# Feed-forward rows turned by VectorE and five DMAs instead of by TensorE

## The reference

```python
def reference(X, W_Q, W_K, W_V, w_gate, w_up, w_down):
    x = X                                             # (8, 2048, 256)
    n = layernorm(x)
    Q, K, V = xpos(n @ W_Q), xpos(n @ W_K, downscale=True), n @ W_V
    p = softmax(Q @ K.T) * 0.9 ** abs(row - column)   # per sequence
    x = x + p @ V
    n = layernorm(x)
    gate, y = fp4_linear(n, w_gate), fp4_linear(n, w_up)      # 704 columns
    return x + fp4_linear(silu(gate) * y, w_down)
```

## Time and profile before

| what | value |
|---|---|
| median of 3 runs | 2549.67 us (2548.38 to 2549.73) |
| profiled execution, first to last instruction | 2546.6 us |
| what lies around this span, against the median | 3.1 us |
| granted TensorE clock, mean over the span | 0.999 of full speed |
| busy: PE, PEld | 2518.4, 2290.0 us |
| busy: DVE, ACT, POOL | 2140.9, 1489.8, 1816.8 us |
| DMA | 203.27 MB, mean 80 GB/s |

### The profile page before, as it was taken

The page is one execution under the profiler, slowest core; times in us unless marked ns, Lnnn a source line. Parts: engine busy times, 40 slices in busy tenths (PEclk is TensorE's granted clock), DMA queues, the critical chain, the costliest instruction groups (busy, mean ns, idle before and its releaser), DMA issues.

```text
span 2546.6 us, 51904 instructions
## 1 busy us (share of the span) xinstructions
PE 2518.4 (99%) x16160; PEld 2290.0 (90%) x16160; DVE 2140.9 (84%) x4759; ACT 1489.8 (59%) x2966; POOL 1816.8 (71%) x1929
## 2 busy tenths in 40 slices
PE   8999999999999999999999999999999999999997
PEld 7888879999999999999999999999999999999996
DVE  8999878888878888888888888888888888888886
ACT  5766565656555655566565656565556655555654
POOL 6999956667767676667766776677666776677665
PEclk9999999999999999999999999999999999999999
DMA  8878511122111311131112111131113111211110
GB/s 285 302 271 299 186 50 30 34 86 66 38 40 45 107 37 42 34 106 42 42 34 91 62 38 40 45 107 39 42 34 106 41 42 34 95 58 38 40 38 22
DMA packets 163473, 203.27 MB, mean 80 GB/s; under 512 B 15184, under 2 KB 116752, under 8 KB 163216
## 3 DMA queue, kind: packets, MB, share of 16 engines
q1 hardware_dynamic: 163216, 200.01, 24.1%
HBM read 103.42 MB, written 77.59 MB: 71 GB/s over the span
## 4 chain that ended last, share of the span: by engine, by line
PE 85%; POOL 0%; DVE 0%; issue 0%; ACT 0%; POOLq 0%
PE score L516 27%; PE acc L655 19%; PE ring L516 19%; PE acc L516 9%; PE ring L622 6%; PE ring L675 3%; PE acc L697 1%; PE ring L613 1%; DVE hT L1226 0%; POOL probs L998 0%; ACT probs L823 0%; ACT hT L793 0%; POOL h_buf L1019 0%; POOL xv L1004 0%; POOL h_buf L1013 0%
## 5 line engine op out<-in xcount | busy, mean ns | idle before, releaser
L516 PE MATMUL score<-keys,q_st 128*128 128x512 f32 x3072 | 733.7, 394 | 3.0 <-ACT probs L823 2.6
L516 PEld LDWEIGHTS score<-keys,q_st 128*128 128x128 f32 x3072 | 567.0, 188 | 117.8 <-issue 3.0
L998 POOL TENSOR_TENSOR probs<-probs,decay 128x512 f32<-128x512 f32 (+3 forms) x416 | 450.7, 1097 | 197.5 <-ACT probs L823 197.5
L655 PE MATMUL acc<-vals,pT 128*128 128x256 f32 x3984 | 554.6, 286 | 0.8 <-DVE pT L1226 0.8
L516 PE MATMUL ring<-w_gu,xqT 128*128 128x512 f32 (+1 forms) x2304 | 509.1, 374 | 0.0
L655 PEld LDWEIGHTS acc<-vals,pT 128*128 128x128 f32 x3984 | 498.1, 189 | 7.3 <-DVE pT L1226 2.0
L516 PEld LDWEIGHTS ring<-w_gu,xqT 128*128 128x128 f32 x2304 | 419.0, 188 | 63.6 <-DVE xqT L1226 0.4
L793 ACT ACTIVATE xqT<-ring 128x256 fp32r<-128x256 f32 x128 | 49.3, 385 | 706.9 <-PE ring L613 706.9
L1239 DVE TENSOR_REDUCE smax<-score 128x1 f32<-128x1024 f32 x256 | 312.8, 1222 | 95.6 <-PE score L516 94.1
L1226 DVE TENSOR_TENSOR pT<-ring,pT 128x512 fp32r<-128x512 f32 (+3 forms) x432 | 248.7, 600 | 66.7 <-ACT pT L793 65.5
L1004 POOL TENSOR_TENSOR xv<-xv,xe 128x256 f32<-128x256 f32 x128 | 94.4, 737 | 269.1 <-DVE xv L1079 269.1
(11 more groups left out here) (133 smaller groups left out, 4470.0 us busy)
## 6 DMA issues: line engine op xcount, KB each, us to landing
k_dram<-keys SPq DMA_DIRECT2D x56, 512.0 KB, 4.5
keys<-k_dram SPq DMA_DIRECT2D x56, 512.0 KB, 7.3
edge<-vals SPq DMA_DIRECT2D x288, 64.0 KB, 2.1
q_raw<-q_dram SPq DMA_DIRECT2D x129, 128.0 KB, 2.6
x_in<-X SPq DMA_DIRECT2D x32, 512.0 KB, 4.5
q_dram<-q_stage SPq DMA_DIRECT2D x32, 512.0 KB, 5.4
x_res<-X SPq DMA_DIRECT2D x128, 128.0 KB, 2.1
out<-x_res SPq DMA_DIRECT2D x128, 128.0 KB, 1.7
```

The source lines that it names most:

```text
L516: mm = pe.matmul(dst, stat(a, k), mov(m, k), start=i == 0, stop=ends and i == n - 1)
L655: mm = pe.matmul(pv_out, pT[g % 2][:, a, j * P:(j + 1) * P], edge[places[m]][:] if kb in edges else vals[m][:, kb, :], start=i == 0, stop= ...
L998: op = pool.tensor_tensor(probs[:, k0:k1], probs[:, k0:k1], decay[:, off + k0:off + k1], ALU.mult)
```

## The change

The transposes of the quantised feed-forward rows leave PE, and with them their two uses of a ring bank in each step. In their place, for tile t:

- DVE in step t+4 (`h_turned_blocks`, behind the lower parts of the last group of probabilities) turns the 128x768 rows in blocks of 32 by 32, each within its own 32 partitions, and writes them to `h_turn`. `hq` has one buffer now, and `h_turn` takes the place of the second.
- SP (`rows_turned`) waits for that, writes `h_turn` to DRAM in one DMA of 384 KB, waits until it has landed, and reads it back into `hqT` in four DMAs of 96 KB, each into 32 partitions, in runs of 768 bytes. This stands in SP's step ahead of the loads of values and edges, of the store and of the load of X, and behind `load_keys` for the second half of the keys and `load_q`.
- ACT in step t+5 makes the upper part from `hqT` in one instruction of 768 columns, behind the first two groups of probabilities instead of ahead of the exponentials.
- DVE in step t+5 makes the lower part in one instruction (`h_lower`), between the lower parts of the first two groups and the maximum of the second half of the scores. Both of its inputs lie in SBUF; before, one lay in PSUM.
- POOL's write to `hq` waits for the turn of the tile before instead of for PE's transposes. Tile 0 takes its 8 blocks as 4 and 4 instead of 2, 3 and 3.

```diff
@@ plan_slots @@
-            for h in range(2):
-                if g == min(max(len(gs) - LATER, 0) + h, max(len(gs), 1) - 1) and has(s - LAG):
-                    take("hT", s - LAG, h)
@@ SP @@
+            def rows_turned(j, t):
+
+                g, i = j * T + t, t % 2
+                sp.wait_ge(h_turned, g + 1)
+                passed()
+                if t > 1 or not isinstance(j, int) or j:
+                    sp.wait_ge(h_split, g - 1)
+                    passed()
+                sp.dma_start(h_dram[i], h_turn.rearrange("p (c r) -> p c r", c=CT)).then_inc(turn_out, 16)
+                sp.wait_ge(turn_out, (g + 1) * 16)
+                for c in range(CT):
+                    sp.dma_start(hqT[i][c * QUAD:(c + 1) * QUAD, :, :], h_dram[i, :, c, :].rearrange("(a i) r -> i a r", a=CT)).then_inc(hqT_back[i], 16)
...
                 if s + 2 <= T or more and not last:
                     load_q(j, s + 2, more)
+                if s >= TURNED or not is_first:
+                    rows_turned(j, s - TURNED)
@@ PE down @@
-                    copied(at, "hT", t, 1)
+                    pe.wait_ge(h_split, tile(at, t) + 1)
@@ ACT @@
             def h_transposed(at, t):
                 if has(at, t):
-                    for h, n in enumerate((CT, HK - CT)):
-                        upper(hT[0][:, h * CT:h * CT + n, :].rearrange("p k t -> p (k t)"),
-                              bank(at, "hT", t, h)[:, 0:n * P], at, "hT", t, h)
+                    act.wait_ge(hqT_back[t % 2], halves(at, t) * CT * 16)
+                    if has(at, t - 1):
+                        act.wait_ge(dn_done, tile(at, t))
+                    act.activation(chunks(hT[0][:]), quads(hqT[t % 2][:]), ACT.Copy).then_inc(h_upper, 1)
...
                 attend(at, s - 1, range(min(n, 2)))
+                h_transposed(at, s - LAG)
@@ DVE @@
+            def h_turned_blocks(at, t):
+                if has(at, t):
+                    dve.wait_ge(hq_ready, tile(at, t) + 1)
+                    if has(at, t - 1):
+                        dve.wait_ge(turn_out, tile(at, t) * 16)
+                    dve.transpose(h_turn.rearrange("p (c k j) -> p k c j", c=CT, j=QUAD), hq.rearrange("p (k c i) -> p k c i", c=CT, i=QUAD)).then_inc(h_turned, 1)
+
+            def h_lower(at, t):
+                if has(at, t):
+                    dve.wait_ge(h_upper, tile(at, t) + 1)
+                    dve.tensor_tensor(chunks(hT[1][:]), quads(hqT[t % 2][:]), chunks(hT[0][:]).bitcast(F32), ALU.subtract).then_inc(h_split, 1)
...
                 attend(at, s - 1, range(min(n, 2)))
+                h_lower(at, s - LAG)
                 maxima(at, s, 1)
...
                 attend(at, s - 1, range(2, n))
-                for h in range(2):
-                    h_transposed(at, s - LAG, h)
+                h_turned_blocks(at, s - TURNED)
                 h_levels(at, s - 3)
```

More of the change, by code:

```diff
@@ L46 @@
 RING = 3
-XR, LAG, LATER = 8, 5, 3
+XR, LAG, TURNED = 8, 5, 4
+QUAD = 32
 W_SLOTS = 3
@@ L89, in groups @@
     bs = blocks_of(t)
-    size = CT if 0 < t < T - 1 else CT - 1
+    size = CT if t < T - 1 else CT - 1
     first = len(bs) % size or size
@@ L170, in build @@
         silu = he
-        hq = [hq_buf[:, i * FT:(i + 1) * FT] for i in range(2)]
+        hq, h_turn = (hq_buf[:, i * FT:(i + 1) * FT] for i in range(2))
         xv, xe, xq = sb("xv", [P, D]), sb("xe", [P, D]), sb("xq", [P, D])
@@ L223, in build @@
         probs = sb("probs", [P, L])
+        hqT = [sb(f"hqT{i}", [P, CT, HK * QUAD]) for i in range(2)]
         score = ctx.enter_context(nc.psum_tensor("score", [P, 4, CH], F32))
@@ L256, in build @@
         hq_step, hv_ready, hg_ready, hq_ready = sem("hq_step"), sem("hv_ready"), sem("hg_ready"), sem("hq_ready")
+        sp_passed, h_turned, turn_out, hqT_back, h_upper, h_split = sem("sp_passed"), sem("h_turned"), sem("turn_out"), [sem(f"hqT_back{i}") for i in range(2)], sem("h_upper"), sem("h_split")
         NSTEP_W, NSTEP_LN2, NSTEP_XQ, NSTEP_HQ = 5, 2, 6, 5
@@ L502, in _ @@
                 step(B - 1, s, False, False)
-            for t in range(T - LAG, T):
-                store(B - 1, t)
+            for s in range(T, T + LAG):
+                if s - TURNED < T:
+                    rows_turned(B - 1, s - TURNED)
+                store(B - 1, s - LAG)
             for i in range(XR):
@@ L663, in attend @@
                         group(at, t, g + 2)
-                    for h in range(2):
-                        if g == min(max(len(gs) - LATER, 0) + h, len(gs) - 1):
-                            later(h)
-            def h_transposed(at, t, h):
-                if has(at, t):
-                    for ks in (range(0, CT), range(CT, HK))[h:h + 1]:
-                        if h == 0:
-                            pe.wait_ge(hq_ready, tile(at, t) + 1)
-                        dst = slot(at, "hT", t, h)
-                        for j, k in enumerate(ks):
-                            mm = pe.transpose(dst[:, j * P:(j + 1) * P], hq[t % 2][:, k * P:(k + 1) * P], ident[:])
-                        mm.then_inc(filled, 1)
             def gate_up(at, t):
@@ L999, in decays @@
                     op.then_inc(decayed, 1)
+                if len(groups(s)) <= 2:
+                    meanwhile()
             def x_quantised(at, t):
@@ L1252, in attend @@
                     lower(pT[g % 2][:, 1, 0:n], bank(at, "pT", t, g)[:, 0:n], pT[g % 2][:, 0, 0:n], at, "pT", t, g)
-            def h_transposed(at, t, h):
+            def h_turned_blocks(at, t):
                 if has(at, t):
-                    for n in (CT, HK - CT)[h:h + 1]:
-                        hi, lo = (hT[i][:, h * CT:h * CT + n, :].rearrange("p k t -> p (k t)") for i in range(2))
-                        lower(lo, bank(at, "hT", t, h)[:, 0:n * P], hi, at, "hT", t, h)
+                    dve.wait_ge(hq_ready, tile(at, t) + 1)
+                    if has(at, t - 1):
+                        dve.wait_ge(turn_out, tile(at, t) * 16)
[4 more added lines that the diff above has]
+                    dve.tensor_tensor(chunks(hT[1][:]), quads(hqT[t % 2][:]), chunks(hT[0][:]).bitcast(F32), ALU.subtract).then_inc(h_split, 1)
             def residual(at, t):
```

23 lines of the change are left out of this document (14 added, 9 removed).

## The result

| what | before | after |
|---|---|---|
| median | 2549.64 us (4 runs, 2548.38 to 2549.73) | 2621.23 us (4 runs, 2618.21 to 2622.3) |
| ratio, with its 95% interval | | 1.0281 (1.0267 to 1.0296) |
| span of the profiled execution | 2546.6 us | 2618.3 us |
| granted TensorE clock, mean | 0.999 | 0.987 |

The change made the kernel 72 us slower. The forecast was +23, with 2618 as its upper end.

A forecast was written before the change was run, and what follows sets the result against it. PE, busy 99%, was taken as the bound. Terms: -84 (transposes) + 63 (third-group waits) + 32 (batch ends) + 12 (tail) = +23 us on the 2546.6 us span; with 3.1 us around it, forecast 2572, range 2522 to 2618.

The forecast's parts named there:

- PE loses the transposes: PE's stream: series of four 0.44 us and of two 0.22, so 0.66 a tile times 128, 84 us saved.
- waits at the third group, and the rest: PE, arriving earlier, waits for DVE's delayed lower part of the third probability group: 63 us, between 21 and 111.
- ends of a batch: Edges queue behind keys and turned rows; PE waits 3.9 us plus clock loss: seven ends, 32 us (18 to 45).
- tail: After the last scores, two ways through DRAM in series, some 21 us for 9: 12 us more (8 to 15).
- the forecast's own list of waits: PE's wait at the third group, tile by tile, from 1.16 us (tile 14) to 0.06 (tile 11); 7.9 a batch.
- d = 0.7: Delay in us of DVE's second maximum caused by the split ahead of it; possible between 0.2 and about 1.3.
- the forecast's rule: DVE instruction with two SBUF inputs and POOL instruction reading SBUF exclude each other throughout; split not 0.95 us beside busy POOL.
- Rival B: Split reaches DVE as POOL passes between instructions, delaying the second maximum only 0.2 to 0.35 us: 2513 to 2542; chance 0.27.
- What DVE and ACT gain and lose: DVE drops 0.68 + 0.43 us, takes a 0.95 us turn where it waited anyway; ACT's single instruction is free.
- The way through DRAM: Turned rows written and read back by SP in 8.0 us, write 3.3; covered by 2.5 us in normal steps.
- rival D: Way through DRAM takes over 10.5 us, late in each step, 100 us and more: 2610 to 2700; chance 0.08.
- the 0.7 us taken: At each batch end, PE's lower clock after the wait for edges costs 0 to 1.5 us more, 0.7 taken.

The follow-up runs named there:

- before_fewer_transposes: Kernel before the change, with PE making only the first transpose of each of its two series of feed-forward rows (four of six dropped); 2511.57 us.
- exps_late: Changed kernel, nothing left out, with six idle ACT copies of 128 columns added ahead of the exponentials; 2604.57 us.
- split_late: Changed kernel with DVE's split of the turned rows moved behind the last group's lower part instead of ahead of the second maximum; 2697.82 us.
- pool_split: Changed kernel with the split (lower part of the turned rows) made on POOL, ahead of its decays, instead of on DVE; 2654.14 us.

## Why the forecast had the right sign and too small a size

The four terms of the sum, with what each came to. The first is read from steps without waits, the third and the fourth from the lengths of the steps above. The second is what is left of the 71.7 us between the two spans, so it holds everything else, and its agreement with the forecast shows nothing by itself.

| term | forecast | found |
|---|---|---|
| PE loses the transposes | -84 | -45 (0.35 x 128) |
| waits at the third group, and the rest | +63 | +66 |
| ends of a batch | +32 | +33.5 |
| tail | +12 | +17.5 |
| sum | +23 | +72 |

**What PE loses** is the step that failed: "That is 0.66 us a tile, times 128 tiles = 84 us." It took the length of two pieces of the chain for what their removal gives. 0.35 us a tile was measured, in steps without waits of the changed kernel and of its variants, and before_fewer_transposes, in which nothing is added and four of six are left out, gave 38 us. In the table this is 39 of the 49 us between the sums. But the same 0.66 us also stood in the times at which PE was to reach the third group, and there it made the waits too long. With 0.36 us for the series of four and nothing for the series of two, the forecast's own list of waits at d = 0.7 gives 5.3 us a batch for 7.9, so 42 us for 63. The step that failed put right alone would have made the sum -45 + 42 + 32 + 12 = +41, 18 us more. The other 31 us are 24 at the waits, 1.5 at the ends of a batch and 5.5 in the tail.

**What the third group waits for** came out as worked in its mechanism: PE waited 54.5 us for pT (forecast 40 to 80), the split's mean was 1.44 us (forecast 1.2 to 2.0), and the second maximum came 0.74 us later, where d = 0.7 was taken. That the second input in SBUF is the cause was shown from both sides (45 us off, 41 on). With this the forecast's rule is borne out as well: the Trainium skill, "SBUF — State Buffer", section "Who interferes with whom", says that a VectorE instruction with two inputs in SBUF contends with a GpSimd instruction that reads SBUF, and that one with at most one input there does not, outside the modes in which VectorE uses two ports. The runs agree, with 1490 ns against 968 for the same columns in the same place. Rival B, POOL clear of the split, would have needed a mean near 0.95.

That the term's size agrees is luck, though: 21 us too much, from the price of the transposes, stood against 24 us that the working didn't have. It reasoned that with ACT's earlier exponentials "PE's scores and POOL's decay have more lead than before", and put their cost at nothing. They bring POOL's decays onto DVE's levels of h, and to put the exponentials back gave 17 us in exps_late. This is a second step that failed. The 17 us don't come through the second maximum, which starts at C+6.51 in exps_late too. PE's waits for pT fell by 6.7 us there, to 47.8, and those for the residual sum from 6.8 to 2.5; the trace doesn't name the rest. Some 7 us of the 66 are not accounted for. One run alone gives the 17, and exps_late moves all that follows the exponentials, so this is no exact split.

By tile the waits are not where the list had them, either. Tile 1 (step 2) waited 2.1 us a batch where 1.04 were forecast, tile 12 (step 13) 0.85 for 0.43, and tile 13 (step 14) for nothing, where 0.79 were forecast.

**What DVE and ACT gain and lose.** The turn took 969 ns (0.95 taken). Its place "where DVE waited anyway" was right for PE's wait, and wrong for what is behind it: split_late and pool_split showed that the residual sum is a second deadline. DVE's busy time from 1000 to 2400 us rose from 1169.5 to 1280.9 us, and ACT and POOL now wait for DVE's mean and variance in most steps.

**The way through DRAM** was covered in normal steps, as worked; ACT waited for its rows 11 times, 41.3 us in all. The write landed after 2.3 us at the median (3.3 taken), so rival D had no ground.

**The end of a batch** went as written in six of seven cases. SP's issues there, to be read beside the earlier trace rows:

```profile
1416.46 3.48 SPq L446 DMA_DIRECT2D keys<-k_dram  x4
1420.14 0.44 SPq L490 DMA_DIRECT2D h_dram<-hq_buf  x1
1430.00 1.74 SPq L493 DMA_DIRECT2D hqT<-h_dram  x4
1432.00 0.36 SPq L455 DMA_DIRECT2D v_raw<-v_dram  x1
1432.41 1.17 SPq L470 DMA_DIRECT2D edge<-vals  x2
```

The write of 384 KB kept SP 9.9 us behind the keys, and PE then stood for the edges:

```profile
1435.75 0.80 PE L687 MATMUL acc<-edge,pT 128*128 128x256 f32 x2 [4.02 <-DMA edge<-vals]
```

4.02 us where 3.9 were forecast. In the same step DVE waited 3.37 us for the turned rows ahead of the split, which is why loading the edges first gained nothing. The clock was dearer than the 0.7 us taken. Windows around it (length; busy of PE, PEld, DVE, ACT, POOL; PEclk; DMA share; GB/s), which answer to the earlier trace rows:

```profile
1431.00:1436.00 5.00, 0.98 (x5) 0.52 (x4) 1.63 (x3) 0.84 (x1) 3.74 (x5) 0.83 0.70 205
1436.00:1438.00 2.00, 2.00 (x11) 2.00 (x11) 1.04 (x2) 0.35 (x1) 0.00 (x0) 0.50 0.29 81
1438.00:1440.00 2.00, 2.00 (x12) 2.00 (x11) 1.61 (x3) 1.74 (x5) 0.00 (x0) 0.50 0.00 0
1440.00:1442.00 2.00, 2.00 (x12) 1.93 (x12) 1.93 (x4) 1.95 (x5) 0.96 (x1) 0.72 0.34 134
1442.00:1446.00 4.00, 4.00 (x23) 3.58 (x22) 3.66 (x11) 2.73 (x6) 3.53 (x6) 1.00 0.42 129
```

PE was busy throughout from 1436 on, for 4 us at 0.50 (1.2 GHz) and 2 at 0.72: 4 x 0.50 + 2 x 0.28 = 2.6 us of work lost. The term came out right because its errors went both ways: only six of the seven ends had the wait, 21.9 us in sum or 3.65 each. 6 x (3.65 + 2.6) = 37.5, less 7 x 0.25 us that a step 0 gains by the transposes (15.68 to 15.43 in before_fewer_transposes), is 36, near the 33.5 of the step lengths. Behind the first batch no wait for edges stands. Its last step has another wait:

```profile
569.88 2.24 PE L687 MATMUL acc<-vals,pT 128*128 128x256 f32 x12 [1.90 <-DVE pT L1248]
```

It is in the 66 us. small_keys has it too (1.94 us), so the 4 MB of keys are not its cause, which stays open.

**The tail** cost 17.5 us, not 12. PE's last down products:

```profile
2593.57 2.55 PE L550 MATMUL acc<-w_dn,hT 128*128 128x256 f32 x15 [2.89 <-DVE hT L1286]
...
2602.28 3.57 PE L550 MATMUL acc<-w_dn,hT 128*128 128x256 f32 x15 [5.74 <-DVE hT L1286]
...
2611.77 3.57 PE L550 MATMUL acc<-w_dn,hT 128*128 128x256 f32 x15 [5.49 <-DVE hT L1286]
```

They come 8.7 and 9.5 us apart, where the earlier trace rows had 4.5, so the two ways through DRAM do stand in series; a way with its parts on ACT and DVE was forecast at 10.7. But each of the last two takes 3.57 us where the last one took 1.99. Windows on these two (columns as above):

```profile
2602.30:2606.00 3.70, 3.70 (x17) 3.69 (x17) 0.82 (x1) 0.00 (x0) 0.00 (x0) 0.50 0.29 111
2611.80:2615.40 3.60, 3.60 (x17) 3.60 (x17) 0.00 (x0) 0.00 (x0) 0.00 (x0) 0.51 0.00 0
```

The granted clock is 0.50, the lower level, behind each of the two gaps of over 5 us. The prediction had the clock only in its term for the ends of a batch; two times 1.6 us is 3 us that it lacked. Another 2.9 us stand in the attention of the last tile, in a gap for which the trace names no releaser and which the kernel before doesn't have:

```profile
2565.22 0.79 PE L687 MATMUL acc<-vals,pT 128*128 128x256 f32 x2 [2.86 <-issue]
```

Its cause is open.

**What beats the kernel before.** Nothing that computes the whole reference. The versions below 2549 us leave out the lower part of h and most of the keys' reload, or four of the six transposes.

## What to carry to other kernels

Price a piece that leaves a pipelined TensorE by how much later it lets the next piece start, in a step in which the engine waits for nothing, and not by its length on the chain; here that is the difference between -84 and -45 us. Use the same price where the piece sets when the engine arrives at its next input, or the error comes back with the other sign (here 21 us). Before an operand moves from PSUM to SBUF in a VectorE instruction, look at what GpSimd does at that moment, and look again at every pair that a change of order brings together, also where the change gives an engine lead. Two costs that hide in the same slack are not a sum: 45 and 20 us alone were 78 together.

## What the runs showed of the hardware that was not expected

- STREAM_TRANSPOSE of 128x768 float32 (L1281) took 966 to 978 ns in the changed kernel, beside a busy POOL, with a mean of 967 to 971 in every kernel that has it.
- The split of 768 columns took from 948 to 2045 ns in one kernel. The spread is larger than the time that it takes alone (0.96 us).
- Of six transposes in PE's stream three cost 0.11 us each (0.36 less 0.02, by 3), and the other three, the first of the one series and both of the other, nothing that could be seen in the length of a step.
- A wait of 4 us cost another 2.6 us through the clock, with PE busy all the time behind it.
